# Attention stage: order of the SyncE transfers, relative tables in four parts, relative operands fetched one unit further ahead

## What is computed

```python
q = _conv1x1(wq, x).reshape(n, NH, HD, H, W)
k = _conv1x1(wk, x).reshape(n, NH, HD, H, W)
v = _conv1x1(wv, x).reshape(n, NH, HD, H, W)
qk = jnp.einsum('nhcij,nhciw->nhijw', q, k) / D
qrq = jnp.einsum('nhcij,chjw->nhijw', q, rq) / D
krk = jnp.einsum('nhcij,chjw->nhijw', k, rk) / D
weight = jax.nn.softmax(qk + Gq * qrq + Gk * krk, axis=3)
out = jnp.einsum('nhijw,nhciw->nhcij', weight, Gv1 * v) + jnp.einsum('nhijw,chjw->nhcij', weight, Gv2 * rv)
```

## Time and profile before

| | |
|---|---|
| median of 3 runs | 7852.92 us (7848.76 to 7871.15) |
| the profiled execution: time, span | 7833.53 us, 7831.8 us |
| attention: first relative product to the last one | 1526.8 to 6152.8 us of the span |
| TensorE busy, whole span | 6488.4 us, 83% |
| VectorE, ScalarE, GpSimd busy | 5358.1, 4715.2, 2470.2 us |
| mean granted TensorE clock | 0.894 of full speed |

### The profile page before, as it was taken

How to read it: one execution, slowest core, us unless ns; L and a number is a source line. 1 busy time by engine, 2 the same in 40 slices (tenths; PEclk the granted TensorE clock), 3 DMA queues, 4 the chain that set the end, 5 groups by cost and what they waited for, 6 DMA issues and landing times. The chain is left out here.

```text
span 7831.8 us, 282296 instructions
## 1 busy us (share of the span) xinstructions
PE 6488.4 (83%) x106442; PEld 5044.5 (64%) x106442; DVE 5358.1 (68%) x20905; ACT 4715.2 (60%) x11171; POOL 2470.2 (32%) x1235
## 2 busy tenths in 40 slices
PE   4999999788898888888898888888888776675648
PEld 3555555477777777777777777777777632232248
DVE  5444444267787777777777777777777698888830
ACT  0444444277787787787787787787787533343310
POOL 0000000034444444444444444444444432232210
PEclk7999999879999999999999999999999998897855
DMA  7555555546656566666656656666666686686522
GB/s 220 202 204 203 203 204 202 147 90 119 117 114 121 112 116 118 114 115 120 113 114 121 114 113 122 112 115 120 111 115 120 148 266 194 202 263 198 177 92 91
DMA packets 1861132, 1148.19 MB, mean 147 GB/s; under 512 B 1162209, under 2 KB 1623649, under 8 KB 1853601
## 3 DMA queue, kind: packets, MB, share of 16 engines
q1 hardware_dynamic: 1670368, 842.63, 49.2%
q10 hardware_dynamic: 188352, 285.27, 10.0%
q0 software_dynamic: 1024, 2.09, 0.1%
HBM read 708.04 MB, written 421.56 MB: 144 GB/s over the span
## 5 line engine op out<-in xcount | busy, mean ns | idle before, releaser
L770 POOL TENSOR_TENSOR att_scores<-att_scores,att_inverse 128x1024 f32<-128x1024 f32 x1024 | 1989.5, 1943 | 2452.0 <-DVE att_inverse L717 2452.0
L732 DVE CUSTOM_DVE_ANT_0 att_scores<-att_ps,att_scores 128x128 f32<-128x128 f32 x8192 | 1819.2, 289 | 1158.7 <-PE att_ps L592 1120.5
L675 ACT ACTIVATE att_scores<-att_scores,att_negmax 128x128 f32<-128x128 f32 x8192 | 2515.0, 394 | 74.7 <-issue 69.5
L581 PE MATMUL att_ps<-att_qk,att_rs 32*128 32x64 f32 x32768 | 2253.6, 300 | 50.8 <-DMA att_qk<-qk 40.5
L592 PE MATMUL att_ps<-att_own 32*128 32x128 f32 x16384 | 1859.1, 328 | 401.3 <-POOL att_rs L765 179.4
L592 PEld LDWEIGHTS att_ps<-att_own 32*128 32x128 f32 x16384 | 1657.3, 197 | 712.4 <-issue 463.3
L581 PEld LDWEIGHTS att_ps<-att_qk,att_rs 32*128 32x128 f32 x32768 | 2073.5, 200 | 52.8 <-issue 43.6
L668 ACT ACTIVATE att_scores<-att_ps 128x1024 f32<-128x1024 f32 x1024 | 1033.7, 1010 | 609.3 <-PE att_ps L581 608.6
L634 PE MATMUL att_ps<-att_scores,att_rv 128*16 128x64 f32 x32768 | 1384.5, 332 | 9.3 <-DMA att_rv<-rv_t 6.3
L715 DVE TENSOR_REDUCE att_total<-att_scores 128x8 f32<-128x1024 f32 x1024 | 1241.5, 1212 | 0.0
L634 PEld LDWEIGHTS att_ps<-att_scores,att_rv 128*16 128x16 f32 x32768 | 1130.9, 121 | 35.1 <-DMA att_rv<-rv_t 12.1
(11 more groups left out here) (147 smaller groups left out, 5173.6 us busy)
## 6 DMA issues: line engine op xcount, KB each, us to landing
qk<-proj_qk_out ACTq DMA_DIRECT2D x64, 2048.0 KB, 8.6
att_qk<-qk SPq DMA_DIRECT2D x512, 256.0 KB, 5.9
att_own<-qk SPq DMA_DIRECT2D x2048, 64.0 KB, 2.5
proj_x<-in_x_dram SPq DMA_DIRECT2D x128, 512.0 KB, 4.3
v_t<-proj_v_out ACTq DMA_DIRECT2D x64, 1024.0 KB, 11.7
att_vt<-v_t SPq DMA_DIRECT2D x256, 256.0 KB, 3.3
att_v<-att_att_v SPq DMA_DIRECT2D x1024, 64.0 KB, 2.5
att_r<-att_att_r SPq DMA_DIRECT2D x1024, 64.0 KB, 2.1
```

What stands on the lines that cost most here:

```text
L581: return pe.matmul(ps[:, 4 + gg, jj * IU:(jj + 1) * IU], rs[32 * g:32 * g + 32, j, :], qk[v % 2][32 * g:32 * g + 32, :, j], start=True, st ...
L675: last = act.activation(scores[v % BUFS][:, i, :], scores[v % BUFS][:, i, :], ACT.Exp, bias=negmax[v % BUFS][:, i:i + 1], scale=-1.0)
L732: last = dve.tensor_tensor_reduce(out=scores[v][:, i, :], in0=ps[:, 2 * (p % 2) + r // HR, (r % HR) * W:(r % HR + 1) * W], in1=scores[v][: ...
L770: pool.tensor_tensor(scores[v][:, rows, :], scores[v][:, rows, :], inverse[v][:, rows].unsqueeze(2).broadcast_to([P, PR, W]), ALU.mult).th ...
```

## The change

The tables are loaded and scaled in quarters (8 columns j of each of the four groups) in place of halves: 32 transfers of 64 KB for each head, and four multiplications on GpSimd of half the size. Each quarter has its own semaphores, and TensorE waits for a quarter ahead of every second round. SyncE's order of issue in a unit is written anew: own half 1, vt 0, (unit 6: gain, quarter 0), store 0, (quarter 1), own half 0 of the next unit, vt 1, (quarter 2), store 1, (quarter 3), qk of unit u+3. The operands `qk` of a unit thus are issued at the end of unit u-3, in place of the start of unit u-2, and unit 2's are loaded ahead of the first unit.

```diff
-        rs_loaded = [s.sem(f"rs_loaded{a}") for a in range(2)]
-        rs_ready = [s.sem(f"rs_ready{a}") for a in range(2)]
+        rs_loaded = [s.sem(f"rs_loaded{a}") for a in range(QUARTERS)]
+        rs_ready = [s.sem(f"rs_ready{a}") for a in range(QUARTERS)]
...
-                        j = g * JG + a * (JG // 2)
+                        j = g * JG + a * JB
...
             def unit(h, k, u, started, left):
+                ahead = ROUNDS * (u + 1)
+                fresh = k == UPH - 2 and left >= 2
                 if started >= 1:
+                    ph, pk = before(h, k, 1)
                     sp.wait_ge(own_done, PIECES * u)
                     load_own(h, k, 1)
-                if left >= 2:
-                    sp.wait_ge(rel_done, ROUNDS * u + ROUNDS)
-                    load_qk(*after(h, k, 2))
-                if started >= 2:
-                    store(*before(h, k, 2), u - 2, 0)
-                if started >= 1:
-                    ph, pk = before(h, k, 1)
                     later(sp, v_done, FILLS * (u - 2) + FILLS // 2)
                     load_v(ph, pk, 0)
                     if pk == 0:
                         later(sp, r_done, FILLS * (u - 2) + FILLS // 2)
                         load_rv(ph, 0)
                         load_rv(ph, 1)
-                fresh = k == UPH - 2 and left >= 2
                 if fresh:
                     load_gain(h + 1)
-                    sp.wait_ge(rel_done, ROUNDS * u + ROUNDS + ROUNDS // 2)
+                    sp.wait_ge(rel_done, ahead + 2)
                     load_relative(h + 1, 0)
+                if started >= 2:
+                    store(*before(h, k, 2), u - 2, 0)
+                if fresh:
+                    sp.wait_ge(rel_done, ahead + 4)
+                    load_relative(h + 1, 1)
                 if left >= 1:
                     sp.wait_ge(own_done, PIECES * u + PIECES // 2)
                     load_own(*after(h, k, 1), 0)
...
+                if fresh:
+                    sp.wait_ge(rel_done, ahead + 6)
+                    load_relative(h + 1, 2)
                 if started >= 2:
                     store(*before(h, k, 2), u - 2, 1)
                 if fresh:
-                    sp.wait_ge(rel_done, ROUNDS * u + 2 * ROUNDS)
-                    load_relative(h + 1, 1)
+                    sp.wait_ge(rel_done, ahead + 8)
+                    load_relative(h + 1, 3)
+                if left >= 3:
+                    sp.wait_ge(rel_done, ahead + ROUNDS)
+                    load_qk(*after(h, k, 3))
...
+            sp.wait_ge(rel_done, ROUNDS)
+            load_qk(0, 2)
...
-                if t % (ROUNDS // 2) == 0:
-                    pe.wait_ge(rs_ready[t // (ROUNDS // 2)], u // UPH + 1)
+                if t % 2 == 0:
+                    pe.wait_ge(rs_ready[t // 2], u // UPH + 1)
...
-                        if k == UPH - 2 and not last and p == 3:
-                            scale_relative(h + 1, 0)
-                        if k == UPH - 2 and not last and p == 7:
-                            scale_relative(h + 1, 1)
+                        if k == UPH - 2 and not last and p % 2 == 1:
+                            scale_relative(h + 1, p // 2)
                         normalise(UPH * h + k, k % BUFS, p)
```

More of the change, by code:

```diff
@@ L539, in unit @@
                 if fresh:
-                    sp.wait_ge(rel_done, ROUNDS * u + 2 * ROUNDS)
-                    load_relative(h + 1, 1)
+                    sp.wait_ge(rel_done, ahead + 8)
[3 more added lines that the diff above has]
+                    load_qk(*after(h, k, 3))
             load_gain(0)
-            for a in range(2):
+            for a in range(QUARTERS):
                 load_relative(0, a)
@@ L550, in _ @@
                 load_own(0, 0, half)
+            sp.wait_ge(rel_done, ROUNDS)
+            load_qk(0, 2)
             for k in range(UPH):
[L552 removed]
+                unit(0, k, k, k, 3)
             with sp.Fori(1, NH - 1) as h:
                 for k in range(UPH):
[L555 removed]
+                    unit(h, k, UPH * h + k, 2, 3)
             for k in range(UPH):
@@ L761, in scale_relative @@
             def scale_relative(h, a):
-                half = slice(a * (JG // 2), (a + 1) * (JG // 2))
+                part = slice(a * JB, (a + 1) * JB)
                 pool.wait_ge(rs_loaded[a], 128 * h + 128)
                 pool.wait_ge(gain_loaded, 128 * h + 128)
-                pool.tensor_tensor(rs[:, half, :], rs[:, half, :], gain[:, :].unsqueeze(2).broadcast_to([P, JG // 2, W]), ALU.mult).then_inc(rs_ready[a], 1)
+                pool.tensor_tensor(rs[:, part, :], rs[:, part, :], gain[:, :].unsqueeze(2).broadcast_to([P, JB, W]), ALU.mult).then_inc(rs_ready[a], 1)
             def normalise(u, v, p):
```

7 lines of the change are left out of this document (3 added, 4 removed).

## The result

The changed kernel takes 7648.78 us (median of 4 runs, 7634.19 to 7655.66) against 7850.84 us (4 runs, 7842.32 to 7871.15) before: a ratio of 0.9737, with a 95% interval of 0.9713 to 0.976, so 202 us or 2.6% less. The forecast was 7520 us, with a range of 7425 to 7650. Direction and range held, the upper end only by 1.2 us, and two of the four runs (7650.06 and 7655.66 us) lie above it: 129 of the 331 us expected didn't come. The execution that was profiled took 7634.19 us, its span is 7632.5 us.

The account below looks back on a forecast made before the run. In the attention TensorE was taken as the bound, losing time to waits for vt and tables and the slower clock. 7833.5 - 488 + 150 + 2 = 7498 us, 7517 with the runs' median, forecast 7520, range 7425 to 7650.

Parts of the forecast that it names:

- The waits for `vt`: TensorE in the attention: all 87 waits, 207.4 us of idle time, go with vt 0 right behind own half 1.
- The waits for the tables: TensorE's 30 waits for scaled tables, 179.4 us, go; each quarter is in time by 2 to 4 us.
- The most that can go, 488 us: Upper limit of the gain in the attention: 468 us over 15 heads and 20 us in the first and last head.
- The new wait on own half 1 of unit 7: TensorE in piece 4 waits 8.1 us, 10.0 with the slower clock; 150 us over 15 heads, 0 to 306.
- the list of 46.5 us: SyncE's issues in unit 6 up to unit 7's own half 1, priced 46.5 us against 31.1 of a unit.
- The loop's branches: TensorE's branch, twice a head, costs 2 x (3.2 + 1.7) = 9.8 us and stays.
- the clock behind the wait: TensorE's slower clock after the new wait on own half 1 costs 1.9 us a head.
- At the start: 32 table transfers in place of 16 ahead of the first qk cost 2 us, between 0 and 7.4.
- SyncE keeps up: Rival: behind the tables nothing waits, issues being faster than in the rows; 7367 us, chance 0.10.
- The queue is heavier: Rival: unit 6's transfers go out as slowly as behind qk, wait at its upper end; 7673 us, chance 0.11.
- SyncE as the bound of every unit: Rival, slower than before: ordinary lists exceed 31.1 us and lengthen each unit; about 7930 us, chance 0.03.
- The page's rule: Skill page's batching advice; its 0.95 us per 64 KB transfer means about 7720 us; the prediction kept 0.5.

Follow-up runs that it names:

- e1: The changed kernel's new order of issue alone, with the tables loaded and scaled in halves as in the kernel before; 7531.68 us.
- e8: The changed kernel without loads and scalings of tables and gains for heads 1 to 15, which use head 0's (computation left out); 7391.49 us.
- e2: The kernel before, in its old order of issue, with only the tables changed to quarters; 7907.37 us.
- e6: The changed kernel with each table transfer of 64 KB cut into two of 32 KB, 64 for a head; 7899.72 us.
- e3: The changed kernel with gains laid out by partition in device memory, so a head's are one transfer in place of eight; 7591.0 us.
- e12: e11 with the qk transfers of the ends of units 3 and 7 issued behind vt 0 of units 4 and 0; 7450.13 us.
- e4: The changed kernel with the qk transfers at the end of unit 6 put behind own half 1 and vt 0 of unit 7; 7618.44 us.
- e10: e7 with the second half of the tables issued ahead of store 1 in place of behind it; 7467.61 us.
- e13: e12 with the qk transfers of the end of unit 6 also put behind vt 0 of unit 7; 7442.73 us.
- e7: e1 with a head's gains as one transfer and GpSimd's two table scalings one normalisation earlier; 7480.64 us.
- e11: e10 with each half of the tables scaled by two multiplications of half the size, each with its own semaphore; 7473.82 us.
- e9: The changed kernel with qk of unit u+2 issued in unit u behind vt 0, in every unit; 7670.67 us.

## Why the prediction was right, and by how much it was off

**The waits for `vt`: right.** All of them went, with the 12 put down to GpSimd. e1 and e8 show that the order alone does this and that ordinary units have slack.

**The waits for the tables: right as such.** 1.9 us are left. That the quarters are in time by 2 to 4 us was too rosy: GpSimd's waits above show them landing late, which is hidden because TensorE is late as well.

**The most that can go, 488 us: nearly right.** e8, without the tables' issues, is 459 us under before. The 29 us between are the branches: a head of e8 takes 261.1 us where 249.1 + 9.8 = 258.9 had been put, 2.2 us more, and its pieces show an excess at the branches alone.

**The new wait on own half 1 of unit 7: right in place and mechanism, mis-sized.** It was there in all 13 heads compared. The step that failed is the term "10.0 us a head, 150 us over 15 heads", priced by the list of 46.5 us from own half 1 to own half 1. The list took 53.6 us in the head shown:

| | predicted | measured |
|---|---|---|
| own half 1 with the tail of `qk` | 6.3 | 6.4 |
| `vt`, twice | 1.1 | 1.1 |
| gains | 3.9 | 5.0 |
| four quarters | 16.4 | 19.6 |
| two rows of stores | 8.2 | 10.1 |
| own half 0 | 4.1 | 5.4 |
| `qk` | 6.5 | 6.0 |
| sum | 46.5 | 53.6 |

Most terms are a little too low. The quarters were priced as own's eight, 4.1 us, since they are as large; they take 4.8 on the mean of 13 heads, nearer to the 5.1 of eight transfers of twice the size, which stood in the prediction as the upper end. The gains and own half 0, read in unit 6 of the kernel before (there 3.9 and 4.1 us on the same mean), take 4.8 and 5.2 here. In e1 the gains take 4.9, so for them it came with the new order; why isn't shown. I also let own half 1 land 9.7 us after its first issue, and it was 7.9 (2383.94 to 2391.83), which gave 1.8 us back.

**What stood ahead of it: missed.** The extra 7 us don't all show as wait on own half 1, because TensorE came to it 5 us later than forecast. That the wait itself came out near the forecast, 9.4 us against 8.1, is partly luck for this reason: both sides were late. TensorE lost 5.7 us on the way, on own half 0 of unit 7 and through ScalarE on the stores of `att_r`. I had asked only for the last item of the list whether it was late and not for those within. So the long list costs 5.7 + 11.8 = 17.5 us a head in place of 10.0. Its total is checked from outside: after less e8 is 257 us, 17.1 us for each of 15 heads.

**The loop's branches: missed.** They were to stay as they were. Each stop is 4.1 us in place of 3.2, and a head loses 11.1 us by them where I had 9.8 (before shows 9.1).

Per head, 7.5 + 1.3 = 8.8 us, 8.7 by the distances of heads; 15 heads make 130 us, and 7649 - 7520 is 129. The rest of the sum held, the clock behind the wait too (1.9 us forecast; pieces 4 and 5 show 1.7 + 0.3). At the start, where 2 us were put, the first own product comes 0.3 us later than before (1575.31 against 1575.01).

**The rivals.** "SyncE keeps up" is what e8 looks like (7391 us, 7367 forecast), but only with the tables' issues gone. "The queue is heavier" was half true: the transfers didn't go out as slowly as behind `qk`, but slower than I priced them, and 7649 lies nearer to its 7673 than to 7520. It deserved more than 0.11. "SyncE as the bound of every unit" is false: in e8 ordinary units wait for nothing. In e2 and e6 the kernel does get slower than before, and by a mechanism that is close to this rival, but nearly all of it in units 6 and 7.

**The page's rule.** The quarter's transfers took 0.61 us each on the mean (19.6 us for 32), between the 0.5 that I kept from the row of `att_r` and the 0.95 of the page, and the total lies between the two sums as well. The number is SyncE's queue's, and in e6 it doesn't change when the bytes halve. The advice in the Trainium skill, "DMA: Bandwidth & Descriptors", section "Measured (HBM→SBUF, 128 partitions, SWDGE, issued from GpSimd)", to batch transfers agrees in direction with e1, e3 and e6: fewer issues were faster each time. I weighed only its figure, and its advice would have been the better guide.

**Left open.** What exactly makes an issue in unit 6 cost 0.5 to 0.75 us rather than less wasn't measured by itself. That a shorter list would take the last wait of e12 away is only what e8 suggests. Halves of the tables in fewer and larger transfers, or a second engine to issue some of them, weren't tried.

## What to carry to other kernels

When all transfers go through one engine's program, price the list between two deadlines, not the transfer: sum its issues against the time of the engine that waits, and ask of every item in it, stores too, when it is wanted. Reordering pays where the list has slack, as it did in the ordinary units, and only shifts the wait where the list itself is too long, as in e4, e10 and e13. Cutting a transfer into smaller ones so that its first part is there sooner costs an issue for each (0.5 us of the kernel's time here) on everything behind it; cut the work on the data instead, and merge small transfers first.

## What the runs showed of the hardware

- An issue on SyncE's queue cost the kernel 0.52 us for 480 more of 32 KB (e6) and 0.3 to 0.55 us for 105 fewer of under 1 KB (e3). In this list size hardly entered: on the mean of 13 heads an issue held SyncE 0.60 us for the gains (under 1 KB) and for 64 KB (after), 0.61 for 32 KB (e6) and 0.66 for 128 KB (before).
- The loop's branch of TensorE depends on what the queues do at that moment. The stop is 3.7 to 4.5 us with `qk` under way (after 4.1; e1, e3, e4, e6, e7, e8, e10 and e11) and 3.2 to 3.4 us without (before, e2, e9, e12 and e13). Two rows, before and after, of the first own product behind a branch:

```profile
2011.94 0.57 PE L592 MATMUL att_ps<-att_own 32*128 32x128 f32 x1 [3.31 <-issue]
```

```profile
2136.16 0.37 PE L601 MATMUL att_ps<-att_own 32*128 32x128 f32 x1 [4.04 <-issue]
```

The trace of the transfers shows a fetch of instructions in it. These rows are of the windows of those two stops (2008.6 to 2012 us before, 2132.1 to 2136.2 us after; packets, MB, share of the engines):

```profile
q8 instruction: 1, 0.02, 2.4%
```

```profile
q8 instruction: 1, 0.02, 1.9%
```

Each of the 26 stops of heads 2 to 14 has one such packet of 16 KB, before and after. Before, it starts 0.2 us into the stop and takes 1.15 us, and TensorE goes on 1.8 us behind its end. After, it starts at 0.6 and takes 1.3, and TensorE goes on 2.15 us behind it; meanwhile some 3350 packets of under 512 bytes are under way, in place of 72. In e9 and e12 the numbers of the packet are back at 0.2 and 1.1. So the fetch is later and slower beside `qk`. The trace doesn't name the engine that a packet of instructions is for; that TensorE waits for this one is an inference from its place in every stop, and what the time behind its end is spent on isn't shown.
